# Two-layer graph network on one core: the last two blocks of layer 1 and the entry into layer 2, put in another order

## What is computed

```python
h = relu(layernorm(x))
ht = (h @ W0).reshape(N, 4, 256)                          # four heads
e = leaky_relu(src[:, :, None] + dst[:, None, :], 0.01) + adj
x1 = x + mean_over_heads(softmax(e) @ ht)                 # layer 1
hidden = relu(layernorm(x1)) @ W1 + b1
A = (adj != 0)
out = x1 + A @ hidden / A.sum(axis=0)[:, None]            # layer 2
```

## Time and profile before

| | us |
|---|---|
| median of 3 runs | 614.47 (613.7 to 615.48) |
| the profiled execution's own time | 613.44 |
| its span, first to last instruction | 611.3 |
| TensorE busy | 532.1 (87%) |
| ScalarE busy | 461.6 (76%) |
| VectorE busy | 456.6 (75%) |

### The profile page before, as it was taken

How to read it: one execution, slowest core, us unless ns; L and a number is a source line. 1 busy time by engine, 2 the same in 40 slices (tenths; PEclk the granted TensorE clock), 3 DMA queues, 4 the chain that set the end, 5 groups by cost and what they waited for, 6 DMA issues and landing times.

```text
span 611.3 us, 9010 instructions
## 1 busy us (share of the span) xinstructions
PE 532.1 (87%) x2991; PEld 304.0 (50%) x2991; DVE 456.6 (75%) x604; ACT 461.6 (76%) x391; POOL 30.9 (5%) x64
## 2 busy tenths in 40 slices
PE   6799669988979898987979898988989799777996
PEld 6333224544536444544545454544545356455885
DVE  5836675887969786979869897888788597363984
ACT  5647775999778977989897997889799696253861
POOL 4000000000000000000000000000000000000211
PEclk9879999999979998999989998999999799888999
DMA  8235151999999999999999999999999999932111
GB/s 321 67 88 200 35 103 32 208 200 217 197 234 196 223 183 220 224 198 235 203 229 200 232 207 218 225 206 230 202 231 205 214 188 202 233 108 83 43 43 43
DMA packets 300319, 108.91 MB, mean 178 GB/s; under 512 B 284748, under 2 KB 295372, under 8 KB 297724
## 3 DMA queue, kind: packets, MB, share of 16 engines
q1 hardware_dynamic: 300296, 108.62, 83.1%
HBM read 30.90 MB, written 6.39 MB: 61 GB/s over the span
## 4 chain that ended last, share of the span: by engine, by line
SPq 34%; PE 24%; ACT 11%; issue 10%; DMA 10%; DVE 8%; DVEq 0%; POOLq 0%; POOL 0%; ACTq 0%
SPq L296 14%; SPq L304 13%; PE ps_relu L804 9%; DMA probs_hi_t<-probs_hi 8%; PE ps_acc L738 7%; ACT logits L529 4%; ACT probs_hi L537 2%; SPq L314 2%; ACT ps_relu L521 2%; DVE probs_lo L943 2%; PE ps_acc L747 2%; DVE logits L934 2%; PE ps_acc L714 1%; PE ps_h L714 1%; DMA hidden_in<-hidden_scratch 1%
## 5 line engine op out<-in xcount | busy, mean ns | idle before, releaser
L738 PE MATMUL ps_acc<-h_w_split,probs_hi_t 128*128 128x512 f16 x1024 | 254.7, 395 | 44.8 <-DMA probs_hi_t<-probs_hi 43.3
L738 PEld LDWEIGHTS ps_acc<-h_w_split,probs_hi_t 128*128 128x128 f16 x1024 | 96.0, 101 | 165.7 <-issue 41.3
L521 ACT ACTIVATE ps_relu<-dst_rows,src_bias 128x2048 f32<-128x2048 f32 x64 | 126.0, 1968 | 63.8 <-DVE small L934 63.6
L934 DVE CUSTOM_DVE_ANT_0 logits<-ps_relu,adj_rows 128x2048 f32<-128x2048 f32 x48 | 109.9, 2290 | 51.8 <-PE ps_relu L724 49.4
L747 PE MATMUL ps_acc<-h_w_split,probs_lo_t 128*128 128x256 f16 x1024 | 122.3, 273 | 0.0
L943 DVE SCALAR_TENSOR_TENSOR probs_lo<-logits,small,probs_hi 128x2048 f16<-128x2048 f32 x48 | 112.7, 2348 | 6.8 <-ACT probs_hi L537 6.8
L747 PEld LDWEIGHTS ps_acc<-h_w_split,probs_lo_t 128*128 128x128 f16 x1024 | 100.1, 98 | 24.1 <-DMA probs_lo_t<-probs_lo 0.4
L537 ACT ACTIVATE probs_hi<-logits,small 128x2048 f16<-128x2048 f32 x48 | 95.5, 1989 | 0.0
L529 ACT ACTIVATE logits<-logits,small 128x2048 f32<-128x2048 f32 x48 | 95.5, 1989 | 0.0
L804 PE MATMUL ps_relu<-hidden_split,mask_columns 128*128 128x512 f32 x256 | 63.0, 407 | 5.1 <-DVE hidden_split L1032 5.1
L804 PEld LDWEIGHTS ps_relu<-hidden_split,mask_columns 128*128 128x128 f32 x256 | 49.6, 195 | 17.0 <-DVE hidden_split L1032 5.8
(11 more groups left out here) (93 smaller groups left out, 380.9 us busy)
## 6 DMA issues: line engine op xcount, KB each, us to landing
adj_rows<-in_adj SPq DMA_DIRECT2D x16, 1024.0 KB, 6.2
dst_rows<-dst_scratch SPq DMA_DIRECT2D x3, 1024.0 KB, 7.0
x_all<-in_x SPq DMA_DIRECT2D x4, 512.0 KB, 5.7
x<-in_x SPq DMA_DIRECT2D x16, 128.0 KB, 2.5
x_scratch<-x SPq DMA_DIRECT2D x16, 128.0 KB, 1.9
hidden_scratch<-hidden SPq DMA_DIRECT2D x16, 128.0 KB, 2.2
out<-out_rows SPq DMA_DIRECT2D x16, 128.0 KB, 1.7
x_in<-x_scratch SPq DMA_DIRECT2D x1, 1792.0 KB, 8.0
```

The costliest lines, as they stand in the source:

```text
L521: nc.scalar.activation(R[:, :], D[:, h, :], ACT.Relu, scale=(1.0 - SLOPE) / SLOPE, bias=src[:, bass.ds(u, 1)]).then_inc(relu_ready, 1)
L738: last = nc.tensor.matmul(ACC[parity][:, :], TA[:, e, b, :], H[:, h, b, :], start=(h == 0 and b == 0), stop=False)
L934: nc.vector.tensor_tensor_reduce(out=logits_of(h, parity), in0=R[:, :], in1=ADJ[:, parity, :], scale=-1.0, scalar=3.0e38, op0=ALU.add, op1 ...
```

## The change

Only orders and places change; every operation is still there once.

- SyncE: `load_hidden(0)` moves from slot (15, 0) to slot (14, 1), with its wait for the low probabilities of unit 59. The wait for all mask transpositions moves to `load_hidden(1)`, which moves from slot (15, 2) to the end of slot (15, 1), next to its old place. Behind the blocks, x1's load of blocks 0 to 13 goes ahead of `store_hidden(14)`.
- ScalarE: `h1_relu(14)` moves from behind the blocks into slot (15, 3), ahead of `hidden_high(1)`, which was in slot (15, 2) and now follows it; `hidden_high(2)` goes ahead of `cast(1, 0, 2)`.
- TensorE: in block 15, `transpose_h1(14)` moves from behind unit 63 to behind unit 62, and `hidden(14)` from between the first two groups of layer 2 to between the high and the low half of unit 63. `transpose_h1(15)` goes six passes earlier, `hidden(15)` 18 passes earlier.
- VectorE: `hidden_low(1)` goes from slot (15, 2) to (15, 3), `hidden(14)` follows it; `degree(1)` and `degree(2)` go from slot (15, 3) to behind `hidden(15)`.

```diff
@@ SyncE, slot @@
-                if final(ib) and h == 0:
+                if isinstance(ib, int) and ib == NB - 2 and h == 1:
                     sp.wait_ge(probs_lo_ready, UNITS - 4)
+                    load_hidden(0)
+                if final(ib) and h == 1:
+                    sp.wait_ge(probs_lo_ready, UNITS)
                     sp.wait_ge(mask_in, 16 * NB)
-                    load_hidden(0)
-                if final(ib) and h == 2:
-                    sp.wait_ge(probs_lo_ready, UNITS)
                     load_hidden(1)
@@ SyncE, behind the blocks @@
             load_hidden(2)
-            store_hidden(NB - 2)
             sp.wait_ge(unit_multiplied, UNITS - 3)
             sp.wait_ge(x1_stored, 16 * (NB - 2))
             sp.dma_start(X1R[:, 0:CH - 1, :, :], paired(x1_dram)[:, 0:CH - 1, :, :]).then_inc(x1_in[0], 16)
+            store_hidden(NB - 2)
             store_x1(NB - 1)
@@ ScalarE, slot @@
                 if final(ib) and h == 2:
                     hidden_high(0)
                     cast(0, 0, 0)
+                if final(ib) and h == 3:
+                    h1_relu(ib - 1)
                     hidden_high(1)
-                if final(ib) and h == 3:
                     cast(0, 1, 1)
@@ ScalarE, behind the blocks @@
-            h1_relu(NB - 2)
+            hidden_high(2)
             cast(1, 0, 2)
-            hidden_high(2)
             cast(1, 1, 3)
             h1_relu(NB - 1)
             hidden_high(3)
@@ TensorE, slot @@
                 multiply(u, k, ib, h, parity)
                 if h == 1 and past(ib, 2):
                     hidden(ib - 2)
+                if final(ib) and h == 3:
+                    hidden(ib - 1)
                 multiply_low(k, h, parity)
-                if h == 3 and past(ib, 1):
+                if h == (2 if final(ib) else 3) and past(ib, 1):
                     transpose_h1(ib - 1)
@@ TensorE, layer 2 @@
             pe.wait_ge(hid_lo_ready, 2)
             aggregate(0, 0, 0, split[1])
-            hidden(NB - 2)
-            aggregate(1, 1, 0, split[1])
+            aggregate(1, 1, 0, split[0])
             transpose_h1(NB - 1)
+            aggregate(1, 1, split[0], split[1])
+            hidden(NB - 1)
             pe.wait_ge(hid_lo_ready, 3)
             aggregate(0, 0, split[1], split[2])
             aggregate(1, 1, split[1], split[2])
             aggregate(2, 2, 0, split[2])
-            hidden(NB - 1)
             aggregate(3, 3, 0, split[2])
@@ VectorE, slot @@
                 if final(ib) and h == 2:
                     hidden_low(0)
                     degree(0)
+                if final(ib) and h == 3:
                     hidden_low(1)
-                if final(ib) and h == 3:
-                    degree(1)
-                    degree(2)
+                    hidden(ib - 1)
@@ VectorE, behind the blocks @@
-            hidden(NB - 2)
             hidden_low(2)
             x1_sum(NB - 1, 1)
             x1_stats(NB - 1)
             norm1(NB - 1)
             hidden(NB - 1)
+            degree(1)
+            degree(2)
             hidden_low(3)
```

## The result

The changed kernel took 605.5 us in the median against 614.09 us, a ratio of 0.9855 with a 95% interval of 0.9827 to 0.9882; on another occasion 604.7 against 613.11, 0.9857 (0.9837 to 0.9878). One of the four runs of the first occasion took 883.48 us at a mean granted clock of 0.559; the ratio leaves it out, and the median of the other three is 605.1 us. The profiled execution took 604.81 us, with a span of 602.7: 8.63 us less than the profiled execution of before.

What follows compares the result with a forecast made beforehand. The DMA queue was taken to bound the time up to S, TensorE's gaps the rest. Gains of 0.8, 0.8, 1.59, 3.07 and 0.55 sum to 6.8 us off 614.47: 607.6 us, range 604.6 to 610.8.

Steps and rivals of the forecast that it cites:

- S: Start of TensorE's first layer-2 pass, 537.62 us in the profile of before; forecast near 536.8.
- T: Start of TensorE's last 200 passes of layer 2, 559.16 us in the profile of before.
- The first load's place: DMA queue, block 14: moving the first load of layer 2's rows lands the second load, and so S, 0.8 us sooner.
- the first rival: Moved load's time won in full: S falls 3.1 us, 605.3, or 603.8 with full clock behind it; chance 0.14.
- Unit 63's transposition: Block 15, DMA: units 60 to 62 land about 3 us later, unit 63 when it did, within 1.5 us of 528.
- Block 14's transposition ahead of unit 63: TensorE waits there for VectorE's norm, some 0.8 us more; unit 63 ends near 535, covered by the gap before S.
- The second rival: TensorE bounds before S: waits for units 60 to 62 bring half clock, 1.7 us each; 609.8 or 611.5; chance 0.16.
- Linear layer, norm, last load: TensorE: block 14's linear layer saves 0.8 us behind S; gaps ahead of block 15's transposition, 1.59, and last passes, 3.07, go.
- The start of the last passes: Behind T: full clock brings only 0.55 us, since pass 9 needs ScalarE's fifth cast.
- with half clock once behind S as now: TensorE behind S: first 12 layer-2 passes take 4.29 us at half clock, as before; assumed in the 6.8 us sum.
- x1's load: Ahead of the last stores: lands near 541, norm's transposition possible at S + 5.0, inside 5.7, at no cost.
- The third rival: x1's load holds up block 15's norm: 609 in the mild form, 616.5 in the full case; chance 0.04.

Runs made afterwards that it cites:

- The two runs that put parts back: Changed kernel with block 14's transposition, relu, linear layer and bias back behind unit 63: 0.9952; changed kernel with both degree sums back ahead of block 15's sum: 0.9917.
- The run in which 3.85 us of idle time stand ahead of S: Changed kernel with block 14's transposition behind unit 63's high half and its linear layer behind the low half: 605.32 us, 0.9866 to the kernel before.
- the kernel whose profile has one such stall less: The kernel before with four already met waits of SyncE added in block 14, nothing else: 613.72 us, 0.9999.

## Why the prediction was right, and where it was off

The forecast was 607.6 us, faster, 604.6 to 610.8; 605.5 lies in the range. Term by term, in the profile: 0.8 forecast and 0.97 measured ahead of S, 5.46 (0.8, 1.59 and 3.07) and 7.15 between S and T, 0.55 and 0.51 behind T. The mechanism was right for the gaps behind S; one term, the clock behind S, was off by a choice, and the reading of S owes something to chance.

- *The first load's place.* 0.8 us were put on S; the profile's S is 0.97 us sooner. From the landing of unit 59's low transposition to that of the second load it took 29.5 to 30.1 us in the four profiles with the load at its old place (29.9 in the kernel before), 28.4 to 29.7 in the eight with it moved (28.7 and 28.9 in the changed kernel's two). The means lie 0.9 us apart, so the size was right, and the first rival, 3.1 us, fell. Counted from the `adj` load, though, S is 2.6 us sooner: most of the rest is the stall near 480 us, missing here, and 1.6 us more ahead of that load cancel it. So the agreement on S within 0.2 us owes something to chance. The queue was also less full than the prediction read it. A share above 1 does not say that it moves data: in the row on 526.2 to 527.8 us it stands at 1.18 with 43 GB/s, and inside the stretch from 500.2 to 508.3 us lies this one, at 54:

```profile
502.50:504.00 1.50, 1.50 (x9) 0.70 (x8) 1.50 (x1) 1.50 (x2) 0.00 (x0) 1.00 1.61 54
```

- *Unit 63's transposition.* It was to land when it did, within 1.5 us of 528. It landed at 526.1 (521.16 + 4.9), 2.2 us sooner than before, and that sign failed. The stall that the prediction kept in place did stay at 526.3 to 527.9 us; in the profile of before it lies ahead of this landing (528.3), in the changed kernel's behind it, and it holds back the store instead.
- *Block 14's transposition ahead of unit 63.* The new wait is where it was put. Its size hangs on the stall: in the first profile unit 63 started 2.8 us after its transposition landed (526.0 to 528.84), since the store that the norm waits for landed 2 us later and not 0.2; in the second profile the store landed 0.2 us later (529.4 and 529.6) and unit 63 started 1.0 us after its transposition, near the 0.8 forecast. It cost nothing, as the cover was there (the run without this wait). The end of unit 63 was forecast near 535 and came at 536.6, level with the second low half. The second rival's mechanism was there, once in each of the two profiles; in the first it took just the gap ahead of S.
- *Linear layer, norm, last load.* The sum came 1.2 us behind S (1.4 forecast), the transposition at S + 4.6 (4.8), x1's load landed at 540.2 (541), spare time ahead of T was 0.9 us (1). The two runs that put parts back show the gap ahead of block 15's norm returning, larger than it was (2.94 and 4.54 us); the one ahead of the last passes stays away in both.
- *The start of the last passes.* 0.55 us forecast, 0.51 measured, with the 1.24 us gap named ahead (about 1.3).
- *The term that was wrong: "with half clock once behind S as now".* T - S was forecast near 16 us (21.54 less 0.8, 1.59 and 3.07) and came out at 14.39. This was a choice, from the row of before; the sentence on full clock, S + 4.1 and a wait of 0.7, was the case that came (S + 4.4 and 0.15). The difference is nearly all of the 1.8 us by which the sum was short (6.8 against 8.63). The run in which 3.85 us of idle time stand ahead of S gave half clock behind it, 18 passes in 6.00 us instead of 4.42, and T - S = 15.6. Why the clock stays full is not shown. In the first profile no idle time stood ahead of S, but in the second 1.53 us did, and in the run with the first load alone moved 3.18 us, with 12 passes in 3.01 us behind them; the kernel before had 2.02 and half clock. The length of the gap ahead of S alone doesn't decide it in these runs.
- *x1's load.* Put at no cost, and the run with it put back shows neither cost nor gain. The third rival fell with it, by little: the store of block 14's hidden rows, issued at 536.96 us, took 3.6 us behind that load and landed 0.2 us ahead of the norm.

## What to carry to other kernels

A transfer moved to another place in a full queue can gain far less than the gap at its old place: here 0.9 us of a 3.1 us load and a 3.31 us gap. Look in the slice of its new place before counting that gap, and at the GB/s there, not at the busy share alone. Where two steps stand ahead of the same late chain, undo each of them alone: the wait that both stand ahead of came back whole with either undone, while the time kept a third and nearly three fifths of the gain. A new wait on an engine cost nothing here because the next thing that engine needed was later still. And a term that hangs on the granted clock is best forecast with both levels in the range: the half clock fell in unit 63 in one execution of the changed kernel and in unit 60 in another.

## What the runs showed of the hardware that was not expected

Stalls of the DMA queue of 0.5 to 1.6 us, at 8 to 95 GB/s, stand beside single packets of the instruction queues. In the profile of before four such packets start near 479.4, 502.4, 504.7 and 525.9 us, and each time the queue falls below 15 GB/s 0.5 to 0.7 us later. The stall near 480 us is there in two of the profiles told of here, each with a packet beside it, and in the others, where it is missing, no such packet starts between 476 and 488 us. The one near 526 us is in the changed kernel's profile as in that of before; in the changed kernel's, in the window from 526.3 to 527.9 us, it is what held the store ahead of the norm back:

```profile
526.30:527.90 1.60, 0.28 (x3) 0.00 (x1) 0.00 (x0) 1.60 (x2) 0.00 (x0) 1.00 1.22 95
```

The Trainium skill, "Runtime: NRT & Kernel Launch", section "Instruction fetch mechanics", calls the cost of crossing into the next code block mostly hidden. The traces don't speak against that as far as the total goes (0.9999 for the kernel whose profile has one such stall less). For the queue in the stretch itself the coincidence does, as what was in flight landed up to 2 us late (the store, 2.0 us behind unit 63's transposition instead of 0.2). Whether the fetch makes the stall was not tried, and what moves the one near 480 us is left open.
